# Attention in an adaptive-layernorm block: pairing wide with narrow key tiles, and summing exponentials ahead of the weighted values

## The reference

```
mod = (silu(c) @ wmod).reshape(4, 6, 1, -1)           # shifts, scales and gates sa, ca, ga, sb, cb, gb
h = layernorm(x) * (1 + ca) + sa
q, k, v = h @ Wq.T + bq, h @ Wk.T + bk, h @ Wv.T + bv  # split into 32 heads
scores = q @ k.T / sqrt(32), masked to the causal half
x = x + ga * ((softmax(scores) @ v) @ Wo.T + bo)
h = layernorm(x) * (1 + cb) + sb
x = x + gb * (a router's 2 best of 4 low-rank experts, weighted, applied to h)
```

## Time and profile before

| | before |
|---|---|
| median of 3 runs | 3147.19 us |
| profiled execution, whole | 3142.79 us |
| its span, first to last instruction | 3140.9 us |
| TensorE matmul busy | 2902.5 us, 92% |
| VectorE / ScalarE / GpSimd busy | 47% / 33% / 44% |
| mean granted TensorE clock | 0.963 of full |

### The profile page before, as it was taken

The page is one execution under the profiler, slowest core; times in us unless marked ns, Lnnn a source line. Parts: engine busy times, 40 slices in busy tenths (PEclk is TensorE's granted clock), DMA queues, the critical chain, the costliest instruction groups (busy, mean ns, idle before and its releaser), DMA issues. The chain is left out here.

```text
span 3140.9 us, 46110 instructions
## 1 busy us (share of the span) xinstructions
PE 2902.5 (92%) x16692; PEld 2043.8 (65%) x16692; DVE 1466.6 (47%) x3029; ACT 1045.4 (33%) x1442; POOL 1374.5 (44%) x701
## 2 busy tenths in 40 slices
PE   3999899989998999699999999999999869999997
PEld 2888788868887888455555555555555456767774
DVE  4121221131213111466666666666666256666664
ACT  1222312121122121155555555555555421112111
POOL 2221322242224121377766776777767613233332
PEclk7999999999999999699999999999999989999997
DMA  6444342333323543735545455555544164434431
GB/s 229 174 167 154 127 161 107 133 134 134 134 107 130 192 167 149 159 85 120 121 110 112 109 112 114 120 121 120 116 112 109 51 177 130 125 107 126 135 114 54
DMA packets 149741, 404.89 MB, mean 129 GB/s; under 512 B 17356, under 2 KB 52612, under 8 KB 148568
## 3 DMA queue, kind: packets, MB, share of 16 engines
q1 hardware_dynamic: 119272, 292.83, 27.5%
q10 hardware_dynamic: 30320, 110.15, 16.7%
HBM read 271.20 MB, written 131.20 MB: 128 GB/s over the span
## 5 line engine op out<-in xcount | busy, mean ns | idle before, releaser
L896 ACT ACTIVATE prob<-ps_s 128x1024 f32<-128x1024 f32 (+3 forms) x768 | 596.3, 812 | 447.3 <-PE ps_s L1017 361.8
L609 PE MATMUL ps_u<-h_hi,w_hi 128*128 128x512 f32 x1536 | 604.7, 394 | 0.0
L609 PE MATMUL ps_u<-h_hi,w_lo 128*128 128x512 f32 x1536 | 600.0, 391 | 0.0
L609 PE MATMUL ps_u<-h_lo,w_hi 128*128 128x512 f32 x1536 | 599.9, 391 | 0.0
L424 POOL TENSOR_TENSOR w_lo<-w_raw,w_hi 128x1024 fp32r<-128x1024 f32 x96 | 231.0, 2407 | 842.3 <-ACT w_hi L471 842.3
L852 POOL TENSOR_TENSOR added<-added,prob 128x2048 f32<-128x2048 f32 (+1 forms) x128 | 550.5, 4300 | 15.4 <-ACT prob L896 15.1
L987 PE MATMUL ps_r<-k_st,q_st 96*128 96x512 f32 (+2 forms) x1536 | 504.7, 387 | 37.0 <-DMA v_sb<-v_tok 27.5
L1017 PE MATMUL ps_s<-q_st,k_st 97*128 97x512 f32 (+2 forms) x1536 | 458.1, 380 | 24.0 <-ACT prob L896 15.4
L939 DVE TENSOR_REDUCE part_high<-ps_r 128x1 f32<-128x512 f32 x512 | 337.7, 687 | 194.3 <-PE ps_r L987 186.2
L546 DVE SCALAR_TENSOR_TENSOR qk_lo<-ps_u,bias_col,qk_hi 128x512 fp32r<-128x512 f32 x128 | 96.1, 751 | 671.9 <-ACT qk_hi L447 671.9
L987 PEld LDWEIGHTS ps_r<-k_st,q_st 96*128 96x128 f32 x1536 | 275.9, 194 | 191.7 <-issue 83.6
(11 more groups left out here) (159 smaller groups left out, 2980.0 us busy)
## 6 DMA issues: line engine op xcount, KB each, us to landing
q_st<-qk_split ACTq DMA_DIRECT2D x90, 512.0 KB, 7.7
k_st<-qk_split ACTq DMA_DIRECT2D x90, 512.0 KB, 13.7
w_raw<-w_cols SPq DMA_DIRECT2D x72, 512.0 KB, 3.5
qk_split<-qk_hi SPq DMA_DIRECT2D x64, 512.0 KB, 2.7
qk_split<-qk_lo SPq DMA_DIRECT2D x64, 512.0 KB, 3.4
xn<-in_L_attn_x SPq DMA_DIRECT2D x8, 2048.0 KB, 13.0
v_tok<-v_out SPq DMA_DIRECT2D x32, 512.0 KB, 2.7
wm<-in_L_wmod SPq DMA_DIRECT2D x8, 2048.0 KB, 8.7
```

What stands on the lines that cost most here:

```text
L609: last = nc.tensor.matmul(ps_u[u % 2][:], w[:, m, k], h[:, k, tok], start=k == 0 and j == 0, stop=k == KT - 1 and j == 2)
L896: nc.scalar.activation(prob[:, buffer_of(t, k), 2 * pair:2 * pair + 2, off:], ps_s[pair][:, :, off:], ACT.Exp, scale=SCALE).then_inc(exp_d ...
```

## The change

Four things are done in `attend`, in one edit.

1. Each slot pairs step `j` from the front with step `tiles - 1 - j` from the back. The widths become 512, 128, 512, 256, 512, 384, 512, 512 for `ch` 1 and 512, 128, 384, 256 for `ch` 0. The order of masks and adds on GpSimd follows; there are 6 adds in place of 5, and only step 7 (now 512 wide, before 256 + 128) goes into `sum_high` by itself. `weigh` now always waits for a mask.
2. The units of a slot alternate: U0 and U2 are the wide step's two pairs of heads, U1 and U3 the narrow step's. Before, U0 and U1 were the first step's, U2 and U3 the second's.
3. `sum_high` and `sum_low` go ahead of `weigh` in the back parts of slots 0 and 1. On ScalarE, `copy_o(t - 1, 0)` moves to behind U0 of slot 2, and the loads for t + 2 to behind U1 of slot 2.
4. The row pass takes rows of both halves in turn, and the four rows left for the next head group's slot 0 are tile 2's, not tile 3's.

```diff
-    steps = [(ch, j) for ch in reversed(range(QC)) for j in range((ch + 1) * CT)]
+    HALVES = tuple(reversed(range(QC)))
+    steps = []
+    for ch in HALVES:
+        tiles = (ch + 1) * CT
+        for j in range(tiles // 2):
+            steps += [(ch, j), (ch, tiles - 1 - j)]
...
-    high = [(i, ch, hs) for i in range(CT, TT) for ch in range(QC) for hs in heads_of(i, ch)]
-    low = [(i, 0, hs) for i in range(CT) for hs in heads_of(i, 0)]
+    high = []
+    for i in range(CT, TT):
+        high += taken_in_turn(*([(i, ch, hs) for hs in heads_of(i, ch)] for ch in range(QC)))
+    low = taken_in_turn([(i, 0, hs) for i in (0, 1) for hs in heads_of(i, 0)], [(3, 0, hs) for hs in heads_of(3, 0)])
+    low += [(2, 0, hs) for hs in heads_of(2, 0)]
...
+        def unit(t, k, pair):
+            return 2 * NSTEP * t + 4 * (k // 2) + 2 * pair + k % 2
...
             for t in range(NG):
+                mask(t, 1)
+                add(t, 2)
                 add(t, 1)
-                add(t, 2)
-                mask(t, 4)
+                mask(t, 3)
                 add(t, 3)
+                add(t, 4)
                 mask(t, 5)
...
             for t in range(NG):
-                for k in range(NSTEP):
-                    exponents(t, k)
...
-                    if k == 3 and t > 0:
+                    if p == 2 and t > 0:
                         copy_o(t - 1, 0)
-                        copy_sums(t - 1, 0)
-                    if k == 4 and 0 < t < NG - 2:
+                    exponents(t, 2 * p + 1, 0)
+                    if p == 2 and 0 < t < NG - 2:
                         act.wait_ge(weighed, PAIRS * t)
                         load(act, t + 2)
-                    if k == 0 and t == 0:
+                    if p == 0 and t == 0:
                         load(act, 2)
+                    exponents(t, 2 * p, 1)
+                    exponents(t, 2 * p + 1, 1)
+                    if p == 0 and t > 0:
+                        copy_sums(t - 1, 1)
+                    if p == 1 and t > 0:
+                        copy_sums(t - 1, 0)
...
-                if 2 * (NSTEP * t + k) > 0:
-                    pe.wait_ge(exp_done, 2 * (NSTEP * t + k - 1) + pair + 1)
+                u = unit(t, k, pair)
+                bank = ps_s[u % 2]
+                if u > 1:
+                    pe.wait_ge(exp_done, u - 1)
...
-                        scores(t, 2 * p + n // 2, n % 2)
+                        scores(t, 2 * p + n % 2, n // 2)
...
                     elif t > 0:
+                        (sum_high if p == 0 else sum_low)(t - 1)
                         weigh(t - 1, PAIRS - HOPS + p)
-                        (sum_high if p == 0 else sum_low)(t - 1)
```

More of the change, by code:

```diff
@@ L16 @@
 from contextlib import ExitStack
+from itertools import zip_longest
 import numpy as np
@@ L663, in attend @@
     RB = 3
-    ADDS = LONG - 3
     HOPS = 2
-    MASKS = QC * CT
-    FIRST = LONG - CT
-    assert QC == 2 and steps[LONG][1] == 0 and steps[FIRST][1] == CT
+    MASKED_STEPS = [k for k, (ch, j) in enumerate(steps) if j >= ch * CT]
+    ADDED_STEPS = (2, 1, 3, 4, 5, 6)
+    ADDS, MASKS = len(ADDED_STEPS), len(MASKED_STEPS)
+    assert QC == 2 and steps[0] == (1, 0) and steps[LONG] == (0, 0) and steps[2][1] < CT
     def heads_of(i, ch):
@@ L673, in heads_of, with taken_in_turn @@
         return [tuple(range(h, h + together)) for h in range(0, HG, together)]
-    high = [(i, ch, hs) for i in range(CT, TT) for ch in range(QC) for hs in heads_of(i, ch)]
-    low = [(i, 0, hs) for i in range(CT) for hs in heads_of(i, 0)]
+    def taken_in_turn(*lists):
+        out = []
+        for group in zip_longest(*lists):
+            out += [use for use in group if use is not None]
+        return out
+    high = []
[3 more added lines that the diff above has]
+    low += [(2, 0, hs) for hs in heads_of(2, 0)]
     EARLY = len(low) - HG
@@ L854, in _ @@
             for t in range(NG):
+                mask(t, 1)
+                add(t, 2)
                 add(t, 1)
-                add(t, 2)
-                mask(t, 4)
+                mask(t, 3)
                 add(t, 3)
+                add(t, 4)
                 mask(t, 5)
-                mask(t, 6)
-                add(t, 4)
+                add(t, 5)
                 mask(t, 7)
[L863 to L867, removed]
+                add(t, 6)
+                for k in range(LONG, NSTEP):
+                    mask(t, k)
         @block.scalar
@@ L898, in _ @@
             for t in range(NG):
[L899 to L901 removed]
+                for p in range(PAIRS):
+                    exponents(t, 2 * p, 0)
+                    if p == 0 and t > 0:
                         copy_o(t - 1, 1)
[L903 to L905 removed]
+                    if p == 2 and t > 0:
                         copy_o(t - 1, 0)
[L907 to L908 removed]
+                    exponents(t, 2 * p + 1, 0)
+                    if p == 2 and 0 < t < NG - 2:
@@ L1026, in weigh @@
                     pe.wait_ge(o_copied, 2 * t + 1)
[L1027 to L1030, removed]
+                pe.wait_ge(masked, masked_upto(t, 2 * p + 1))
                 for k in (2 * p, 2 * p + 1):
                     ch, j = steps[k]
-                    off, end = offset(k), j == (ch + 1) * CT - 1
+                    off, end = offset(k), k in (LONG - 1, NSTEP - 1)
                     for h in range(HG):
                         part = slice(h * HD, (h + 1) * HD)
-                        last = nc.tensor.matmul(ps_o[part, off:], v_sb[t % SLOTS][:, j, part], prob[:, buffer_of(t, k), h, off:], start=j == 0, stop=end)
+                        last = nc.tensor.matmul(ps_o[part, off:], v_sb[t % SLOTS][:, j, part], prob[:, buffer_of(t, k), h, off:], start=k in (0, LONG), stop=end)
                 last.then_inc(weighed, 1)
@@ L1058, in sum_high @@
                     nc.tensor.matmul(bank_of(use)[h * HD:(h + 1) * HD, :], ones[:], added[t % 2][:, h], start=True, stop=False)
[L1059 to L1062, removed]
+                k = LONG - 1
+                off = offset(k)
+                for h in range(HG):
+                    last = nc.tensor.matmul(bank_of(use)[h * HD:(h + 1) * HD, off:], ones[:], prob[:, buffer_of(t, k), h, off:], start=False, stop=True)
                 last.then_inc(sum_done, 1)
```

42 lines of the change are left out of this document (25 added, 17 removed).

## The result

The changed kernel takes 3173.0 us, the median of 4 runs (3170.62 to 3178.37), against 3148.2 for the kernel before on the same chip. The ratio is 1.0083, 95% interval 1.0068 to 1.0097: slower by some 26 us by the ratio, 25 by the medians. I had forecast 3167 and slower.

A forecast was written before the change was run, and what follows sets the result against it. Front parts bound by three engines handing work around, back parts by TensorE alone. -1.24 + 1.65 + 0.40 = +0.81 us a head group, +23.5 over 29 groups, some 0.3 gained in three others: forecast 3167 us, range 3130 to 3190.

The forecast's parts named there:

- Slots 0, 1 and 4: Front parts with a wide and a narrow step: U3 no longer waits, gaining 0.61, 0.40 and 0.35 us.
- Rival one: Front parts win: U3's freedom shortens slots 0, 1 and 4 to 3.4 us, -0.59 a group, 3130 us; chance 0.24.
- Slots 2 and 3: ScalarE's DMA hole ahead of U2 and wide slot 3: TensorE waits over 1 us, loss 1.65 us a head group.
- my lower bound: Slots 2 and 3: with TensorE's wait hidden, wide slot 3 and slot 2's shorter back part still lose 0.4 us.
- The shift's wait: Slot 0: the shift has over 1 us more to land since slot 5 grows, so its remaining wait goes.
- Back parts: TensorE's back parts: new widths +0.65 us a head group, sums first may give back some 0.2; taken as +0.40.
- Edits at nothing: GpSimd's adds and masks, `weigh`'s mask waits, copies of sums and rows in turn: no time change.
- The clock: Rival: TensorE standing over 1 us in slot 3 drops the clock, +3 us a group, about 3255 us; chance 0.02.
- VectorE: Rival: banks not yet reduced hold front parts of slots 0, 1 and 4; gain halves, 3188 us; chance 0.12.
- fronts of slots 0, 1, 4 and 5: Front parts: gains in slots 0, 1 and 4 with slot 5's loss of 0.12, together -1.24 us a head group.
- The head groups without loads: Three head groups issue no loads, so have no hole in ScalarE's queue; gain some 0.3 us each.

The follow-up runs named there:

- the experiment on the units: Changed kernel with new step pairs kept but units in the old order (wide pair, wide pair, narrow pair, narrow pair), against the kernel before: 3200.2 us, ratio 1.0166.

## Why the prediction was right

**Slots 0, 1 and 4** were forecast to gain 0.61, 0.40 and 0.35. On average they went from 4.55, 4.26 and 4.28 to 3.74, 3.79 and 3.90: 0.81, 0.47 and 0.38. The spacing U0 to U2 held, and the experiment on the units shows that it is alternation that frees U3. Rival one, where these slots fall to 3.4, is out. Part of slot 0's gain is the shift's wait: I had taken 0.46 of it off the one group that I read, and the average group still had some.

**Slots 2 and 3**, the term that decided: forecast +1.65, measured 9.52 to 11.08, +1.56. The order that I gave (copy, U1, hole, U2, wait of TensorE, wide slot) stands in ScalarE's rows, but the DMAs are issued beside the copy already, and U2's exponential starts 6.1 behind the slot's start and not 6.45. The hole of the group that I read was 0.11 over the mean (2.64 against 2.53), not 0.15. Taking the hole away gave back 1.16 of it. The rest, 0.40, is my lower bound, the wide slot 3 and the shorter back part of slot 2.

**The shift's wait** went as forecast. But its cause was left open. In the kernel before it is not the loads, most likely the short slot 5. With the loads on SyncE behind the stores, the end of their transfer takes its place.

**Back parts** are mis-sized, and nearly as much as the front parts above: I took +0.40 and they are +0.71. The run with weighted values first parts the two things that I had added. The widths alone are worth +1.00 where I had +0.65. Sums first take 0.29 off, and I had taken 0.25. The widths cost more because my slope of 1.28 ns a column was too flat. Its lower point, 1.03 for 384 columns, was slot 5's, where a half ends and TensorE waits for its own matmuls; its upper ones have no such wait. Between 640, 768 and 896 columns outside slot 5 (1.21, 1.43 and 1.64) it is 1.7 ns a column, and 128 columns less in `sum_high` gave 0.21. So slot 5 with 1024 columns is 2.10 and not 1.85.

**Edits at nothing** held: no wait of `weigh` for a mask appears among the waits, and no run shows row order to be worth anything.

**The clock** I had put at nothing in the sum, with a rival at 0.02 that gave it 3 us a group. It did fall in slot 3, where the rival said, but in five groups of 29 and for 9.9 us in all, a tenth of the rival's size. The changed kernel's trace and those of four versions with the loads on ScalarE have 21 falls, all of them in slot 3. With the loads on SyncE there was one in the steady stretches of three traces, behind a wait for the shift; in the version with the old order of units, and in the four traces made of the kernel before, none. What exactly sets one off no run shows: it fell behind waits of 0.94 to 1.25 us in slot 3, and it did not fall behind others of 1.27 and 1.28.

**VectorE** did not halve the gain, so its rival is out for this kernel. But the row pass's weight loads now wait for it 91 us where it was 62, and its wait in the kernel before without the hole shows that it stands next in line.

So the number came out right in part by luck. Outside the falls a head group takes 0.67 more, not 0.81: fronts of slots 0, 1, 4 and 5 -1.60 (forecast -1.24), slots 2 and 3 +1.56 (+1.65), back parts +0.71 (+0.40). The head groups without loads (0, 30 and 31) gained 4.2 us together, where I had 1; a piece of it is a fall of the clock at 2488 us in the kernel before. Both leave the stage some 15 us longer in place of the 22 that I forecast. The clock's 9.9 us make that 25.4, and the stages outside add 5.5 of which I knew nothing. The mechanism that decides the sign, the hole ahead of a wide slot, is shown; the closeness of 3167 to 3173 is not its merit alone.

## What to carry to other kernels

Work that an engine's own queue issues (here seven DMAs, 2.5 us of hole) costs only what stands behind it in that queue and cannot wait. Before reordering work around it, list what the next slots ask of that engine; or take the issue to an idle queue first and then reorder. A change that shortens one slot also shortens the time that small transfers had to land in.

## What the runs showed that I had not expected

- A 2 KB transfer issued while 3.5 MB are on their way waited for their end: moving the loads about 4 us ahead cut that wait from 18.3 us to 0.2 in all.
- The last stage, with the same code, took from 647.6 us (granted clock 0.93) to 657.5 (0.91) in the traces of this study; the lowest clock, 0.90, went with 656.9. So the time of a single execution can move by up to 10 us against what its attention stage shows.
- TensorE's clock fell to 1.2 GHz for 3.4 to 6.8 us at a time in the changed kernel's steady stretch, in which it never stood longer than 1.3 us.
- Where TensorE waits for its own last matmul, it stands 0.18 us at the end of a back part, and 0.18 (kernel before) or 0.33 (weighted values first) in the middle of one.
